# A two-layer graph transformer on one core: P.V of all heads in one block, shares of groups 0 and 1 transposed together

## The reference, cut to what matters

```
x = x + layer0(relu(layernorm(x)), adj + adj)
x = x + layer1(relu(layernorm(x)), adj)

q, k, v = h @ Wq.T, h @ Wk.T, h @ Wv.T + bv        # 12 heads of 32 channels
scores  = q @ k.T * 384 ** -0.5 + bias             # a row that is zero all over gets weight 0
out     = softmax(scores) @ v
return out @ Wo.T + bo
```

## Time and profile before

| | |
|---|---|
| median of three runs | 1602.06 us |
| profiled execution, its own time | 1602.71 us |
| its span in the trace | 1600.8 us |
| granted TensorE clock | 0.997 of 2.4 GHz |
| busiest engine | TensorE, 97% of the span by modelled ends |
| VectorE, ScalarE, GpSimd | 86%, 86%, 82% |
| DMA queue of SP | 257 MB, 70% of 16 engines' time |

### The profile page before, as it was taken

The page is one execution under the profiler, slowest core; times in us unless marked ns, Lnnn a source line. Parts: engine busy times, 40 slices in busy tenths (PEclk is TensorE's granted clock), DMA queues, the critical chain, the costliest instruction groups (busy, mean ns, idle before and its releaser), DMA issues.

```text
span 1600.8 us, 45924 instructions
## 1 busy us (share of the span) xinstructions
PE 1550.4 (97%) x13184; PEld 1402.1 (88%) x13184; DVE 1372.1 (86%) x5190; ACT 1368.9 (86%) x4297; POOL 1320.1 (82%) x1673
## 2 busy tenths in 40 slices
PE   5999999999999999999999999999999999999996
PEld 5888998889889889888898899898898899898895
DVE  5898888888888888888888888888888888888895
ACT  5888888888889888888888888888888888888885
POOL 3788888888888888888888888888888888888885
PEclk9999999999999999999999999999999999999999
DMA  8677777676677676776776776766767767767664
GB/s 246 133 158 158 164 168 175 147 173 155 159 177 168 152 177 150 163 176 148 167 160 157 175 169 157 172 155 154 180 156 164 158 162 164 176 153 171 153 137 113
DMA packets 132538, 260.22 MB, mean 163 GB/s; under 512 B 30400, under 2 KB 58560, under 8 KB 132288
## 3 DMA queue, kind: packets, MB, share of 16 engines
q1 hardware_dynamic: 132288, 257.28, 70.4%
HBM read 26.48 MB, written 12.58 MB: 24 GB/s over the span
## 4 chain that ended last, share of the span: by engine, by line
PE 71%; SPq 14%; DMA 8%; DVE 2%; issue 2%; ACT 2%; POOL 0%; POOLq 0%; ACTq 0%; DVEq 0%
PE misc_bank L714 19%; PE misc_bank L758 12%; PE probT_bank L652 10%; PE misc_bank L733 10%; PE score_bank L640 8%; DMA stack<-split_qk 8%; SPq L242 7%; SPq L232 6%; PE values_bank L660 6%; PE values_bank L669 2%; PE misc_bank L694 2%; PE values_bank L746 2%; DVE split_qk L512 1%; ACT split_qk L435 1%; ACT prob L389 1%
## 5 line engine op out<-in xcount | busy, mean ns | idle before, releaser
L389 ACT ACTIVATE prob<-neg,guard 128x256 f32<-128x256 f32 x1536 | 764.2, 510 | 2.8 <-DVE guard L535 2.7
L308 POOL TENSOR_TENSOR half<-neg 128x256 f32<-128x256 f32 x768 | 550.9, 738 | 35.5 <-DVE guard L535 8.1
L535 DVE CUSTOM_DVE_ANT_0 neg<-score_bank,bias 128x256 f32<-128x256 f32 x1536 | 568.7, 416 | 7.6 <-PE score_bank L640 6.6
L401 ACT ACTIVATE probT<-probT_bank 128x512 f32<-128x512 f32 x512 | 290.8, 597 | 71.3 <-PE probT_bank L652 71.1
L640 PE MATMUL score_bank<-stack 96*128 96x256 f32 x1536 | 316.4, 308 | 2.9 <-DMA stack<-split_qk 1.7
L389 ACT ACTIVATION_READ_ACCUMULATOR prob<-neg,guard 128x1 f32 x1536 | 309.2, 201 | 0.0
L652 PE MATMUL probT_bank<-identity,prob 128*128 128x128 f32 x2048 | 307.3, 273 | 1.0 <-ACT prob L389 0.7
L313 POOL TENSOR_TENSOR half<-half 128x512 f32<-128x512 f32 x192 | 247.1, 1287 | 15.1
L640 PEld LDWEIGHTS score_bank<-stack 96*128 96x128 f32 x1536 | 221.1, 191 | 30.5 <-DVE guard L535 26.1
L652 PEld LDWEIGHTS probT_bank<-identity,prob 128*128 128x128 f32 x2048 | 242.4, 141 | 5.9 <-ACT prob L389 1.1
L435 ACT ACTIVATE split_qk<-misc_bank 128x512 fp32r<-128x512 f32 x192 | 114.6, 597 | 105.7 <-DMA stack<-split_qk 80.4
(11 more groups left out here) (92 smaller groups left out, 3988.3 us busy)
## 6 DMA issues: line engine op xcount, KB each, us to landing
stack<-split_qk SPq DMA_DIRECT2D x768, 192.0 KB, 3.7
moved<-blocks SPq DMA_DIRECT2D x1024, 64.0 KB, 2.0
rows<-x SPq DMA_DIRECT2D x32, 384.0 KB, 5.2
out<-rows SPq DMA_DIRECT2D x32, 384.0 KB, 2.8
bias<-adj SPq DMA_DIRECT2D x32, 256.0 KB, 5.2
neg<-w0q SPq DMA_DIRECT2D x1, 576.0 KB, 4.4
prob<-w0k SPq DMA_DIRECT2D x1, 576.0 KB, 6.4
probT<-w0v SPq DMA_DIRECT2D x1, 576.0 KB, 7.4
```

Of the source, the lines that this page charges most:

```text
L308: nc.gpsimd.tensor_tensor(half[:, step % GROUP, :, :], n[:, :, 0:N // 2], n[:, :, N // 2:N], ALU.add).then_inc(half_done, 1)
L389: nc.scalar.activation(prob[:, step % PROB, q, :], neg[:, step % NEG, q, :], ACT.Exp, scale=-1.0, bias=guard[step // GROUP][:, step % GROU ...
L401: nc.scalar.activation(probT[:, n % PROBT, :, :].rearrange("p a b -> p (a b)"), probT_bank[n % 2][:, :], ACT.Copy).then_inc(act_copy_done, 1)
L535: nc.vector.tensor_tensor_reduce(out=neg[:, step % NEG, q, :], in0=score_bank[step % 2][:, q * N:(q + 1) * N], in1=bias[u.t % GRAPHS][:, q ...
```

## The change

All three groups' P.V now stands in one block, in the slot after the scores: first the moved heads and group 1 into the two halves of one bank, then group 2 into half of the other. The parts are dealt anew: part 0 is groups 0 and 1 together, part 1 is group 2. The lists of all five engines are written in another order to go with it, TensorE's slot begins at another point of the cycle, both value projections stand next to each other, the bias is loaded for `project` instead of `norm`, and block copies wait for the first two groups' P.V instead of all. No arithmetic is added or removed.

```diff
         def part_groups(part):
-            return slice(0, GROUPS, 2) if part else slice(1, 2)
+            return slice(2, 3) if part else slice(0, 2)
...
             def move_blocks(u, to):
-                sync.wait_ge(heads_ready, u.before(1).count(PARTS, 2))
+                sync.wait_ge(heads_ready, u.before(1).count(PARTS, 1))
...
-                    (stack_quadrant, attend, 2), (stack_quadrant, attend, 3), (load_rows, norm, 0),
-                    (load_bias, norm, 0), (move_blocks, attend, 1), (move_blocks, attend, 3),
-                    (move_blocks, attend, 0), (stack_quadrant, project, 0), (stack_quadrant, project, 1),
-                    (move_blocks, attend, 2), (store, output, 0),
+                    (stack_quadrant, attend, 3), (load_rows, norm, 0), (load_bias, project, 0),
+                    (move_blocks, attend, 0), (move_blocks, attend, 3), (move_blocks, attend, 2),
+                    (stack_quadrant, project, 0), (stack_quadrant, project, 1), (move_blocks, attend, 1),
+                    (stack_quadrant, project, 2), (store, output, 0),
...
             def copy_sharesT(u, part):
-                bank = values_bank[1][:, :] if part else values_bank[1][:, N:2 * N]
-                nc.scalar.activation(sharesT[:, 0:1 + part, :].rearrange("p a n -> p (a n)"), bank, ACT.Copy
+                bank = values_bank[1][:, N:2 * N] if part else values_bank[1][:, :]
+                nc.scalar.activation(sharesT[:, 0:2 - part, :].rearrange("p a n -> p (a n)"), bank, ACT.Copy
...
             def scale_heads(u, part):
-                width = (1 + part) * N
+                width = (2 - part) * N
...
-            def weigh_values(u, part):
-                if part == 0:
-                    pe.wait_ge(values_done, u.count(TILES, TILES))
-                    pe.wait_ge(act_copy_done, u.count(TURNED, GROUP))
-
-                    pe.wait_ge(sharesT_done, u.before(1).count(PARTS, 2))
-                    mm = weigh_turned(u, 1, values_bank[1][:, 0:N])
-                else:
-                    pe.wait_ge(act_copy_done, u.count(TURNED, TURNED))
-                    for moves in blocks_moved:
-                        pe.wait_ge(moves, u.count(16 * QUADS, 16 * QUADS))
-
-                    pe.wait_ge(heads_done, u.before(1).count(PARTS, 2))
-                    weigh_moved(u, values_bank[0][:, 0:N])
-                    mm = weigh_turned(u, 2, values_bank[0][:, N:2 * N])
-                mm.then_inc(heads_ready, 1)
+            def weigh_values(u, _):
+                pe.wait_ge(values_done, u.count(TILES, TILES))
+                for moves in blocks_moved:
+                    pe.wait_ge(moves, u.count(16 * QUADS, 16 * QUADS))
+                pe.wait_ge(act_copy_done, u.count(TURNED, GROUP))
+
+                pe.wait_ge(heads_done, u.before(1).count(PARTS, 1))
+                weigh_moved(u, values_bank[0][:, 0:N])
+                weigh_turned(u, 1, values_bank[0][:, N:2 * N]).then_inc(heads_ready, 1)
+                pe.wait_ge(act_copy_done, u.count(TURNED, TURNED))
+
+                pe.wait_ge(sharesT_done, u.count(PARTS, 1))
+                weigh_turned(u, 2, values_bank[1][:, 0:N]).then_inc(heads_ready, 1)
...
             def transpose_shares(u, part):
-                pe.wait_ge(heads_done, u.count(PARTS, 1) if part else u.before(1).count(PARTS, 2))
-                for g in range(1 + part):
+                if part == 0:
+                    pe.wait_ge(heads_done, u.before(1).count(PARTS, 2))
+                else:
+                    pe.wait_ge(sharesT_done, u.count(PARTS, 1))
+                for g in range(2 - part):
...
             def stages(attend, project, output, norm):
-                    (transposes, output, 8), (weigh_values, output, 0), (project_v, attend, 1),
+                    (scores, attend, 4), (project_keys, project, 0), (scores, attend, 5), (weigh_values, output, 0),
```

More of the change, by code:

```diff
@@ L325, in split_heads @@
                 pool.wait_ge(heads_done, u.count(PARTS, part + 1))
-                groups, heads = part_groups(part), headsT[:, 0:1 + part, :]
+                groups, heads = part_groups(part), headsT[:, 0:2 - part, :]
                 nc.gpsimd.tensor_scalar(headsT_high[:, groups, :], heads, 1.0, 0.0, ALU.mult, ALU.add
@@ L407, in spread_shares @@
                 act.wait_ge(sharesT_ready, u.count(PARTS, part))
-                wide = shares[:, 0:1 + part, :, :]
+                wide = shares[:, 0:2 - part, :, :]
                 tiny = share[:, part_groups(part), :, :].rearrange("p g q (h a) -> p g (q h) a", a=1)
-                nc.scalar.activation(wide, tiny.to_broadcast([P, 1 + part, TILES * GROUP, HEAD]), ACT.Copy
+                nc.scalar.activation(wide, tiny.to_broadcast([P, 2 - part, TILES * GROUP, HEAD]), ACT.Copy
                                      ).then_inc(spread_done, 1)
@@ L554, in find_share @@
                 dve.wait_ge(exp_done, u.count(2 * HEADS, 2 * GROUP * (g + 1)))
-                dve.wait_ge(spread_done, u.before(1).count(PARTS, 1 if g == 1 else 2))
+                dve.wait_ge(spread_done, u.before(1).count(PARTS, 2 if g == 2 else 1))
                 nc.vector.reciprocal(inverse[:, g, :, :], sums[u.k % 2][:, heads, :]).then_inc(guard_done, 1)
@@ L570, in scale_heads @@
                 dve.wait_ge(heads_split_done, u.count(PARTS, part))
-                width = (1 + part) * N
-                nc.vector.tensor_tensor(headsT[:, 0:1 + part, :].rearrange("p a n -> p (a n)"),
-                                        values_bank[0 if part else 1][:, 0:width],
-                                        sharesT[:, 0:1 + part, :].rearrange("p a n -> p (a n)"), ALU.mult
+                width = (2 - part) * N
+                nc.vector.tensor_tensor(headsT[:, 0:2 - part, :].rearrange("p a n -> p (a n)"),
+                                        values_bank[part][:, 0:width],
+                                        sharesT[:, 0:2 - part, :].rearrange("p a n -> p (a n)"), ALU.mult
                                         ).then_inc(heads_done, 1)
@@ L610, in slot @@
                     (shift_rows, project, 0), (add_value_bias, attend, 1), (negate_scores, attend, 0),
[L611 to L616 removed]
+                    (rows_low, project, 0), (rows_low, project, 1), (negate_scores, attend, 1),
+                    (find_share, output, 2), (negate_scores, attend, 2), (negate_scores, attend, 3),
+                    (turn_blocks, attend, 0), (turn_blocks, attend, 1), (negate_scores, attend, 4),
+                    (turn_blocks, attend, 2), (turn_blocks, attend, 3), (scale_heads, output, 0),
+                    (negate_scores, attend, 5), (qk_low, project, 0), (negate_scores, attend, 6),
+                    (negate_scores, attend, 7), (scale_heads, output, 1), (qk_low, project, 1),
                     (find_share, attend, 0), (negate_scores, attend, 8), (negate_scores, attend, 9),
[L618 removed]
+                    (qk_low, project, 2), (result, output, 0), (statistics, norm, 0), (negate_scores, attend, 10),
                     (find_share, attend, 1), (result, output, 1), (statistics, norm, 1), (mean, norm, 0),
@@ L739, in transpose_shares @@
                 pe.wait_ge(spread_done, u.count(PARTS, part + 1))
[L741 to L742 removed]
+                if part == 0:
[3 more added lines that the diff above has]
+                for g in range(2 - part):
                     s = shares[:, g, :, :].rearrange("p a b -> p (a b)")
[L744 removed]
+                    at = N * (1 if part else g)
                     for q in range(TILES):
```

53 lines of the change are left out of this document (22 added, 31 removed).

## The result

The changed kernel takes 1578.22 us (median of four runs, 1577.92 to 1581.69) against 1601.69 us (1599.18 to 1602.61) for the kernel before: a ratio of 0.9861, 95% interval 0.9843 to 0.9879. The profiled execution's span went from 1600.8 to 1576.1 us, 24.7 less, where 31 were forecast.

What follows compares the result with a forecast made beforehand. TensorE, 97% busy, was taken as the bound, with an irregular transfer-loop loss and a fixed query wait. Terms -0.24 + 0.05 - 0.30 = -0.49 us a slot, -31 us over 63 slots: 1602.7 - 31 - 0.65 = 1571 us, range 1549 to 1600.

Steps and rivals of the forecast that it cites:

- the one run of 48 matmuls: Sign on TensorE's timeline: P.V as one run of some 2.8 us, with scores on both sides.
- The undisturbed slot: Sign on TensorE: a slot without the irregular loss takes 23.7 to 23.8 us, from 23.94 before.
- the wait of the first queries: Sign on TensorE: the queries' first load still waits 0.3 to 0.4 us a slot.
- the wait on split_qk: Sign on TensorE's weight loads: under 10 us in all, from 22.7; over 20 would speak for rival A.
- rival A: Transfer loop keeps its loss because the last split waits for its ScalarE copy: -0.19 us a slot, 1590 us; chance 0.22.
- TensorE's order: TensorE's stages: one P.V block saves 0.34 us a slot, other transitions cost 0.10: -0.24, between -0.54 and -0.24.
- fixed wait before the queries: TensorE's wait for rowsT_low: from 0.30 to 0.35 us a slot, bounds 0 and 0.5, so +0.05.
- loop through SP: SP's stack copies, ScalarE's overwriting of split_qk, third queries: loss falls from 0.395 to 0.10 us a slot, so -0.30.
- The room: Slack for SP's stack copies between last split and third queries: grows by about 1.1 us a slot.
- B: Merged P.V block waits in its middle for ScalarE's copy of the first shares: slower, 1628 us; chance 0.12.
- C: TensorE's gain is eaten: query wait grows by 0.34, transfer loop gives back only 0.10: 1602 us; chance 0.06.
- the tail: End of the kernel, where the last unit's remaining stages run alone as before: 2 us allowed.

Runs made afterwards that it cites:

- e_split: The changed kernel with P.V split in two again, group 2 moved behind the second keys: 1578.82 us, ratio 0.9869 to the kernel before.
- b_store_between: The kernel before with only the store moved, from ahead of the third quadrant's stack copies to between third and fourth: 1618.28 us, ratio 1.0112.
- e_store_mid: The changed kernel with the store moved back ahead of the third stack quadrant, from between third and fourth: 1560.53 us, ratio 0.9732 to the kernel before.
- b_rows_together: The kernel before with the row transposes side by side on TensorE and the row copies side by side on ScalarE: 1601.57 us, ratio 0.9987.

## Why the prediction was right in its sum and wrong in its steps

Sign and size came out, 1578 for 1571, but two steps were wrong in opposite directions, by -0.32 and +0.48 us a slot. That the sum is only 0.09 off is luck. Of the signs that the prediction named, the one run of 48 matmuls came (2.73 us). The undisturbed slot is 23.36 and not 23.7 to 23.8, the wait of the first queries is gone and not 0.3 to 0.4, and the wait on split_qk is 27.7 us, not under 10 and over the 20 that was to speak for rival A.

| term, us a slot | forecast | measured |
|---|---|---|
| TensorE's order | -0.24 | -0.31 |
| fixed wait before the queries | +0.05 | -0.27 |
| loop through SP | -0.30 | +0.18 |
| sum | -0.49 | -0.40 |

**TensorE's order: right.** Entry, exit and block came as the rows said (0.33, 0.34 and 2.73 for 2.79), and transposes that meet pay, as chosen. The measured value is what the undisturbed slot's 0.58 leaves when the wait's share is taken off; no run has it alone, but e_split gives about 0.3 for the one block where the prediction had 0.34.

**The fixed wait: wrong.** The step "The wait would be 0.5 instead of 0.30" set 9.0 us of chain against 8.5 of TensorE. The wait on rowsT_low fell by 17.0 us, 0.27 a slot. In the slot shown the shift ends 5.06 us behind the second output projection's start (767.18 to 772.24), not 5.25, and from `normalise` to the copy of T9 ScalarE takes 2.44 (772.28 to 774.72), not the 2.75 of the summed durations. With 0.60 for that copy and 0.36 for T11 the chain is 8.5 us, and TensorE's own work 8.67 (767.18 to 775.85). The overlap of ScalarE's instructions was seen in the working and not taken off in full; the bound of 0 was the right end.

**The loop: wrong, the failed step.** "Only the third quadrant and the store trade places, so the length from the first issue to the last landing is unchanged": it is not unchanged. With a store, SP's first stack copy to TensorE's third queries took 18.35 us before (mean of the slots with a store) and 18.99 in the changed kernel; b_store_between shows that the trade alone costs 18 us and e_store_mid that undoing it brings them back. The room, "about 1.1 us", was over-read too. The third queries stand 0.34 us later behind the first scores, not 0.65 (11.46 to 11.80 in undisturbed slots): the query wait that went away, 0.30, lay ahead of them, so the error on the fixed wait is one here as well. In slots with a store the split ends 0.31 us earlier, counted to the next first scores, where 0.66 less the slot's 0.2 was forecast, so the room there grew by 0.65 us; and SP uses nothing of the split's share, busy with its block copies until 837.69 in the slot shown. Of the loss, 0.33 us a slot before and 0.47 after lie between the first scores and the third queries, where the wait on split_qk is; the rest is not traced. With the store in its old place the loss would have been 0.30, from 0.39: even then -0.09, not -0.30.

**The sum itself was the third error.** Savings on TensorE and a shorter loop were added, but in slots that the loop sets, a TensorE saving only lengthens TensorE's wait: e_split and b_rows_together show 0.3 and 0.2 us of the undisturbed slot that leave the time as it is. Rival A (the loop keeps its loss, 1590) was nearest in kind; its reason was not the cause: in all 56 slots the third split starts right behind the negated scores, 0.4 us or more after ScalarE's copy. Rivals B and C did not come: no weight load waits for sharesT (one matmul does, 0.4 us), and the query wait shrank.

**The ends.** 2 us were allowed for the tail, and the sum of 31 left them out. From the first scores of the first unit to those of the last the time fell by 28.4 us, ahead of and behind that it rose by 3.7.

## What to carry to other kernels

A DMA list is a chain of its own. Here the store directly ahead of the copies that everyone waits for was on the path with its bytes, and cost 18 us; between one quadrant ahead of them and right behind them lay 2 us in one kernel and 6 in the other. Before adding up savings, look at which loop sets the period (the chain's share by engine says it), and count savings on other engines only as far as that loop has slack. When the slots of a mean differ, sort them by what they contain; here "with a store" and "without" named the suspect before any experiment.

## What the runs showed of the hardware

VectorE's small shift (128x2) ends with GpSimd's instruction beside it. In the kernel before it runs 0.96 us next to a GpSimd addition that started just ahead of it and takes 1.01; in the changed kernel its neighbour takes 0.74 and it takes 0.69:

```profile
783.92 1.01 POOL L341 TENSOR_TENSOR rows<-rows,o_bias 128x384 f32<-128x384 f32 x1
```
```profile
794.81 0.74 POOL L308 TENSOR_TENSOR half<-neg 128x256 f32<-128x256 f32 x1
...
794.88 0.69 DVE L497 SCALAR_TENSOR_TENSOR shift<-mean_var,inv_dev 128x2 f32<-128x2 f32 x1
```

In all 56 slots of units 4 to 59, in both kernels, the shift ends 14 to 21 ns behind that instruction. The Trainium skill, SBUF — State Buffer, SBUF: two separate sides, says that a VectorE operation with two inputs in SBUF and a GpSimd operation that reads SBUF hold a shared port pair in turn, the later one blocked until the first is done; these rows agree. So the reorder seems to have made the shift 0.27 us shorter by what stands beside it on GpSimd; no run changed that alone.
